# A four-layer graph network on one core: a dense copy of the layer 0 sums, compared numbers in PSUM, twelve gather buffers

## The reference

```python
h = relu(layernorm(x)); x = x + L0(h)   # recv = segment_sum(edge_attr, dst); relu([recv, h, u] @ W1 + b1) @ W2 + b2, 1024 hidden
h = relu(layernorm(x)); x = x + L1(h)   # attention over the edges of a node (max, exp, sums)
h = relu(layernorm(x)); x = x + L2(h)   # degree-scaled sums of node rows, once forward and once backward, two 128x128 products
h = relu(layernorm(x)); x = x + L3(h)   # sums of edge_weight * h[src] by dst, mean, product, layer norm, relu
```

## Time and profile before

| | us |
|---|---|
| median of three runs | 9123.56 (9121.67 to 9123.86) |
| the profiled execution | 9116.86, its span 9115.2 |
| nodes of layer 0 | about 1765 to 2610 |
| layer 2 forward, gathers | 5384 to 6177 |
| layer 2 backward, gathers | 6783 to 7452 |
| layer 3, gathers | 8205 to 8904 |
| PE, DVE, ACT, POOL busy | 7221, 6414, 3251, 4580 |

### The profile page before, as it was taken

One profiled execution on the slowest core, in us unless ns is written; L12 is line 12 of the kernel. 1 busy time (PEld: TensorE's weight loads), 2 busy tenths in 40 slices (PEclk: granted clock), 3 DMA queues, 4 the chain that ended last, 5 costly groups with the idle time before them and its releaser, 6 DMA issues. The chain is left out here.

```text
span 9115.2 us, 230332 instructions
## 1 busy us (share of the span) xinstructions
PE 7221.3 (79%) x60850; PEld 5827.1 (64%) x60851; DVE 6414.1 (70%) x20871; ACT 3251.0 (36%) x9379; POOL 4580.0 (50%) x5503
## 2 busy tenths in 40 slices
PE   4855577799968888888887987776987775997777
PEld 4755566544446666666676766665876664886665
DVE  5999888611147777777776776666776666876667
ACT  3533322222223333333334530005640015668881
POOL 2000477100037777777733557773557752557771
PEclk7985799899977777777788999998999997999996
DMA  0000366400014444444435876676766654776663
GB/s 22 2 2 1 96 140 140 114 23 24 25 48 107 106 107 105 107 105 106 106 121 194 290 237 192 190 179 204 280 244 191 193 169 165 282 281 175 184 184 102
DMA packets 645064, 1262.09 MB, mean 138 GB/s; under 512 B 126526, under 2 KB 183433, under 8 KB 644569
## 3 DMA queue, kind: packets, MB, share of 16 engines
q1 hardware_dynamic: 424337, 704.50, 23.6%
q0 software_dynamic: 199040, 544.46, 22.4%
q10 hardware_dynamic: 21452, 10.20, 0.4%
HBM read 780.96 MB, written 477.75 MB: 138 GB/s over the span
## 5 line engine op out<-in xcount | busy, mean ns | idle before, releaser
L1063 PE MATMUL PS<-w,GS 128*128 128x128 f32 x12176 | 1636.6, 283 | 499.8 <-DVE AREA L1008 229.0
L1063 PEld LDWEIGHTS PS<-w,GS 128*128 128x128 f32 x12176 | 1457.8, 192 | 678.9 <-DVE w L967 444.5
L1171 POOL DMA_INDIRECT GS<-t1d,KI x1564 | 1492.7, 954 | 488.0 <-issue 461.5
L1188 POOL DMA_INDIRECT GS<-xbuf,KI x964 | 1028.4, 1067 | 360.9 <-issue 173.6
L967 DVE TENSOR_TENSOR w<-IO,KI 128x512 f32<-128x512 f32 (+1 forms) x1355 | 808.7, 597 | 421.9 <-issue 411.1
L2419 DVE TENSOR_SCALAR AREA<-PS,IP 128x512 bf16<-128x512 f32 x1116 | 837.4, 751 | 219.7 <-PE PS L2429 115.9
L2441 PE MATMUL PS<-AREA 128*128 128x128 bf16 x13392 | 934.7, 220 | 56.4 <-POOL AREA L2399 56.4
L2441 PEld LDWEIGHTS PS<-AREA 128*128 128x128 bf16 x13392 | 843.5, 98 | 196.6 <-issue 66.1
L2399 POOL TENSOR_TENSOR AREA<-AREA,w 128x192 int32<-128x192 int32 x1116 | 547.8, 504 | 615.7 <-PE PS L2441 330.2
L2381 ACT ACTIVATE GS<-PS 128x512 f32<-128x512 f32 x1116 | 666.4, 597 | 393.5 <-PE PS L2441 393.2
L1188 POOL DMA_INDIRECT GS<-pbuf,XR x558 | 594.0, 1065 | 208.1 <-issue 100.5
(11 more groups left out here) (412 smaller groups left out, 13040.0 us busy)
## 6 DMA issues: line engine op xcount, KB each, us to landing
xbuf<-GS SPq DMA_DIRECT2D x1116, 256.0 KB
XR<-in_edge_attr SPq DMA_DIRECT2D x780, 256.0 KB
pbuf<-AREA SPq DMA_DIRECT2D x482, 256.0 KB
GS<-t1d,KI POOLq DMA_INDIRECT x1564
GS<-xbuf,KI POOLq DMA_INDIRECT x964
GS<-pbuf,XR POOLq DMA_INDIRECT x558
AREA<-t2d ACTq DMA_DIRECT2D x121, 64.0 KB
keyd<-AREA POOLq DMA_INDIRECT x482
```

What stands on the lines that cost most here:

```text
L1063: i = e.matmul(PS[:, s % 3, 0:128], feats(s)[0:m, r, 0:D], SELW[s % 3][0:m, width * r:width * r + 128], start=(r == 0), stop=(r == 3))
L1171: e.indirect_dma_start(GS[0:m, s, r, 0:wide], None, table, bass.IndirectOffsetOnAxis(ap=idx[0:m, c:c + 1].bitcast(U32), axis=0)).then_inc( ...
L1188: e.indirect_dma_start(GF[:, 512 * s:512 * s + 512], None, buf, bass.IndirectOffsetOnAxis(ap=idx[:, b:b + 1].bitcast(U32), axis=0)).then_i ...
```

## The change

Three edits. In `l0_nodes` DVE copies a group's 512 strided sums into a dense buffer `AGT` (two of them, in turn), and the products of PE with the first half of `W1` read that buffer. In the summing passes the numbers 0 to 127 are copied once per phase into PSUM bank 7, and `sel` reads them there. The gathers of the summing passes go round 12 slots, six in `GF` as before and six in `R`, and the loops of DVE, PE and ACT run over 12 batches per turn.

```diff
-    def batches(e, nb, step):
+    def batches(e, nb, step, un=UN):
...
-            if s == 0:
-                held[0] = ranges(e, part, it * (2 * UN), 2 * UN)
-            return held[0][2 * s:2 * s + 2]
+            if s % UN == 0:
+                held[0] = ranges(e, part, it * (2 * un) + 2 * s, 2 * UN)
+            return held[0][2 * (s % UN):2 * (s % UN) + 2]
...
+        num = PS[:, 7, 0:width] if not srel else IO[:, 0:width]
+
         def sel(e, s, kl):
-            return e.tensor_tensor(SEL[s % 3], IO[:, 0:width].unsqueeze(1).to_broadcast([128, 4, width]),
+            return e.tensor_tensor(SEL[s % 3], num.unsqueeze(1).to_broadcast([128, 4, width]),
...
+            if not srel:
+                e.tensor_copy(num, IO[:, 0:width])
...
+    GRING = 12
+
+    def gslot(s):
+
+        return GF[:, 512 * s:512 * s + 512] if s < 6 else R[:, 512 * (s - 6):512 * (s - 5)]
...
-                s = b % UN
-                if b >= UN:
-                    e.wait_ge(bd, b - UN + 3)
-                e.indirect_dma_start(GF[:, 512 * s:512 * s + 512], None, buf,
+                s = b % GRING
+                if b >= GRING:
+                    e.wait_ge(bd, b - GRING + 3)
+                e.indirect_dma_start(gslot(s), None, buf,
...
+        AGT = [B0[:, LISTEND + 4096 + 512 * i:LISTEND + 4608 + 512 * i] for i in range(2)]
+        ag = p.sem("ag")
...
+                e.wait_ge(ag, g + 1)
...
-                    e.matmul(PS[:, m % 2, 0:4 * n].rearrange("h (j p) -> h j p", j=4), W1S[:, 0, 128 * m:128 * m + 128],
-                             jp(AB[:, 0, :], g), start=True, stop=False)
+                    e.matmul(PS[:, m % 2, 0:4 * n], W1S[:, 0, 128 * m:128 * m + 128], AGT[g % 2][:, 0:4 * n],
+                             start=True, stop=False)
...
+            def sums(g):
+                n = grows[g]
+                if g >= 2:
+                    e.wait_ge(ph, 8 * (g - 1))
+                e.tensor_copy(AGT[g % 2][:, 0:4 * n].rearrange("f (j p) -> f j p", j=4), jp(AB[:, 0, :], g)).then_inc(ag, 1)
+
...
+            sums(0)
             copy0(0)
             for g in range(NG):
                 if g + 1 < NG:
+                    sums(g + 1)
                     copy0(g + 1)
...
-                  ready, 16, ACC, weight=weight)
+                  ready, 16, ACC, weight=weight, un=GRING)
```

More of the change, by code:

```diff
@@ L925, in gnn, with unit_ranges @@
     NIT = NBF // UN
-    def batches(e, nb, step):
-        n = nb // UN
+    def batches(e, nb, step, un=UN):
+        n = nb // un
         with e.Fori(0, n) as it:
[L931 to L936, removed]
+            for s in range(un):
+                step(it * un + s, s, it, False)
+        for s in range(nb % un):
+            step(n * un + s, s, n, n * un + s == nb - 1)
+    def unit_ranges(e, nb, part, un=UN):
         held = {}
-        n = nb // UN
+        n = nb // un
         def get(b, s, it, last):
@@ L943, in get, with edge_pass @@
                 return ranges(e, part, 2 * b, 2)
-            if s == 0:
-                held[0] = ranges(e, part, it * (2 * UN), 2 * UN)
-            return held[0][2 * s:2 * s + 2]
+            if s % UN == 0:
+                held[0] = ranges(e, part, it * (2 * un) + 2 * s, 2 * UN)
+            return held[0][2 * (s % UN):2 * (s % UN) + 2]
         return get
-    def edge_pass(p, nb, tail, width, part, keys, feats, ready, rstep, ACC, weight=None, count=False, srel=False):
+    def edge_pass(p, nb, tail, width, part, keys, feats, ready, rstep, ACC, weight=None, count=False, srel=False, un=UN):
         acc, mmd, oh, bd, dv, kx = (p.sem(n) for n in ("acc", "mmd", "oh", "bd", "dv", "kx"))
@@ L988, in _ @@
             e.nop().then_inc(acc, 3)
-            get = unit_ranges(e, nb, part)
+            get = unit_ranges(e, nb, part, un)
             if count:
@@ L1038, in step @@
                     i.then_inc(sr, 1)
-            batches(e, nb, step)
+            batches(e, nb, step, un)
             for q, w_ in (((nb - 2) % 3, wq), ((nb - 1) % 3, wp)):
@@ L1176, in gather @@
         return ready
+    GRING = 12
+    def gslot(s):
+        return GF[:, 512 * s:512 * s + 512] if s < 6 else R[:, 512 * (s - 6):512 * (s - 5)]
     def gather_groups(p, bd, buf, idx, nb):
-        ready = [p.sem(f"g{s}") for s in range(UN)]
+        ready = [p.sem(f"g{s}") for s in range(GRING)]
         @p.on("gpsimd")
@@ L1184, in _ @@
             for b in range(nb):
-                s = b % UN
-                if b >= UN:
-                    e.wait_ge(bd, b - UN + 3)
-                e.indirect_dma_start(GF[:, 512 * s:512 * s + 512], None, buf,
+                s = b % GRING
+                if b >= GRING:
+                    e.wait_ge(bd, b - GRING + 3)
+                e.indirect_dma_start(gslot(s), None, buf,
                                      bass.IndirectOffsetOnAxis(ap=idx[:, b:b + 1].bitcast(U32), axis=0)
                                      ).then_inc(ready[s], 16)
-            for s in range(UN):
-                e.wait_ge(ready[s], 16 * ((nb - 1 - s) // UN + 1))
+            for s in range(min(GRING, nb)):
+                e.wait_ge(ready[s], 16 * ((nb - 1 - s) // GRING + 1))
         return ready
@@ L1278, in l0_nodes @@
         H0T = [B0[:, LISTEND + 3072 + 512 * i:LISTEND + 3584 + 512 * i] for i in range(2)]
-        assert LISTEND + 4096 <= NC
+        AGT = [B0[:, LISTEND + 4096 + 512 * i:LISTEND + 4608 + 512 * i] for i in range(2)]
+        ag = p.sem("ag")
+        assert LISTEND + 5120 <= NC
         HT = [HTS[:, 528 * i:528 * i + 528].rearrange("p (j f) -> p j f", j=4) for i in range(2)]
@@ L2671, in aggregate @@
         ready = gather_groups(p, p.sem("bd"), buf, idx, nb)
-        edge_pass(p, nb, 128, 128, part, keys, lambda s: GF[:, 512 * s:512 * s + 512].rearrange("p (r f) -> p r f", r=4),
-                  ready, 16, ACC, weight=weight)
+        edge_pass(p, nb, 128, 128, part, keys, lambda s: gslot(s).rearrange("p (r f) -> p r f", r=4),
+                  ready, 16, ACC, weight=weight, un=GRING)
         for k in ("vector", "tensor"):
```

## The result

| | us |
|---|---|
| before, beside it | 9122.74 (9121.67 to 9123.86, 4 runs) |
| changed | 8960.60 (8957.45 to 8978.58, 4 runs) |
| ratio | 0.9826, 95% interval 0.9809 to 0.9843 |
| profiled execution of the changed kernel | 8957.86, its span 8956.2 |

A forecast was written before the change was run, and what follows sets the result against it. PE was taken to bound layer 0's nodes, POOL's gathers layer 2, with slot waits added in layer 3. Terms 173 - 1 + 61 + 58 + 90 = 381 us off 9116.9 give 8736, median 8742 us; range 8710 to 8860.

The forecast's parts named there:

- the long loop is fetched anew: Rival: DVE's longer loop in the summing passes is refetched each turn and pauses; 8780 to 8855 us, chance 0.17.
- The pause: At the head of DVE's loop turns, a refetch was priced at 2.2 us more per turn.
- The cover: Twelve batches take DVE 13.8 us and POOL 15.1, so 1.3 us of a refetch pause per turn is free.
- The sum: Refetch cost in the summing passes: 0.9 us per turn, 113 us for all three passes, some 38 for one.
- the refetch at its dearest: Upper end of the range: refetched DVE loops in the summing passes bring the kernel to 8860 us at most.
- The rival for slower: Refetch pauses of 4.3 us per turn in all three summing passes eat the whole gain; 9335 at 6 us; chance 0.02.
- Dense sums: Nodes of layer 0: a dense operand saves PE 0.887 us per piece, 173 us, less 1 us for the first copy.
- Numbers in PSUM: Summing passes: one SBUF operand fewer for DVE shortens POOL's gathers to 0.957 us, 0.11 us less per batch, pace 1.257.
- Twelve slots: Summing passes: later gathers come six places earlier, 7.5 us per pass; layer 3 also loses its waits for a slot.
- The forecast's own sum: Whole kernel: all terms together save 381 us, giving a median of 8742 us; chance 0.63.

The follow-up runs named there:

- e13: Changed kernel with 48 one-element memsets on VectorE ahead of the loop of layer 2 backward and 48 ahead of layer 3's; 8732.7 us, ratio 0.9576.
- e9: Changed kernel with 6 memsets on VectorE ahead of the loop of layer 2 backward and 48 ahead of layer 3's; 10630.9 us, one run, beside 10446.6.
- e10: Changed kernel with 120 memsets on VectorE ahead of the loop of layer 2 backward and 68 ahead of layer 3's; 10427.8 us, one run, beside 10446.6.
- e12: Changed kernel with 48 memsets ahead of each loop of layer 2 backward and layer 3, compared numbers read from SBUF again; 10252.6 us, ratio 0.9814.
- e16: Changed kernel with a ring of six buffers and loops of six batches, dense sums and numbers in PSUM kept; 8808.3 us, ratio 0.9661.
- e11: Changed kernel with nine buffers and loops of nine batches, ranges loaded three batches at a time, no memsets; 10348.9 us, ratio 0.9905.
- e14: Changed kernel with nine buffers and loops of nine batches, ranges of all nine in one load; 8941.3 us, ratio 0.9805.

## Why the prediction was wrong

**The step that failed** is the rival "the long loop is fetched anew": "The trace has no such pause; the nearest rows are the idle time at a turn's head, 1.4 us, and at the first entry of a pass, 2.2". The mechanism was named, the queue with its packets too, but it was given 0.17 and three parts of its price were off:

- The pause. It was taken at 2.2 us more per turn for want of a row. The heads of the turns idle 6.6 us in the median, against 1.4 to 1.6 in the same pass of e13: some 5.0 us more. Three of a turn's five packets lie inside the pause, in the turn shown at 6963.4, 6965.3 and 6967.9 us, one after another, which fits blocks that are asked for only when they are missed.
- The cover. "1.3 us of a pause is free" counted DVE's and POOL's times per turn with PE at full clock. A turn takes 20.8 us for POOL's 15.1: 5.7 lost, so nothing of the 5.0 was free. In the turn shown PE runs empty, its granted clock is still at 0.50 for some six microseconds after it has work again, and the comparisons at 6973.42, 6975.12 and 6976.83 are 1.7 us apart where POOL needs 1.257. No run separates the clock's share from that of the pause.
- The sum. One pass was priced "some 38" us; it cost 836.2 - 613.4 = 223. With the pause alone put right, the prediction's own formula gives 40 x (5.0 - 1.3) = 148, an estimate; the other 75 are the cover. The 223 are the whole miss: 8960.6 - 223 = 8738.

The range closed at 8860, "the refetch at its dearest", with 2.2 us as the dearest pause; the forecast plus the true cost of one pass, 8742 + 223 = 8965, lies 105 us above that. The rival for slower asked for a pause of 4.3 us in all three passes; it was longer than that, but in one pass of three. That two passes were spared is a matter of their place, which the prediction did not look at (shown for layer 3 by e9 and e10; no run moved the loop of layer 2 forward); it counted 269 rows in the body, where the compiled loop has 331 instructions.

**Dense sums**: right, sized 172, measured 179 by the first gather of layer 1. A piece went from 2.66 to 1.71 us, 0.95 less where 0.887 was priced; over 192 pieces that would be 12 us, of which 7 are seen. That the copy is hidden is right. What the Trainium skill says of a stride of 4 float32 being free (SBUF — State Buffer, DMA port swizzle) does not hold for this operand of PE; its other clause, two hits per line, agrees with the factor of two, since a step of four float32 leaves one.

**Numbers in PSUM**: right. The gathers' mean went from 1064 and 1079 ns to 957 with no gather above 1054 (the median was 957 before, too), and in e12, with the operand in SBUF, the means are back at 1062 and 1081. e16 against before gives their worth with six slots: 47, 47 and 31 us.

**Twelve slots**: e13 against e16 gives 22, 8 and 54 us. The 7.5 us per pass fit layer 2 backward; in layer 3 the real waits for a slot went, as said, and in layer 2 forward 14 us more came, most of it at the end of the pass, which had been left "as they are": from the 482nd gather to the last it takes 121 us in e16 and 111 in e13.

**The forecast's own sum** of 8742 was right for the mechanism without the fetches: 8733. In part that is luck, since the terms err both ways: the dense sums gave 7 us more than their term and layer 2 forward 8 more, layer 2 backward (669 to 613) 2 less and layer 3 (700 to 614) 4 less.

## What to carry to other kernels

A hardware loop's price depends on its compiled length and on where it lands: at 331 instructions of VectorE the same loop cost 613 or 836 us per pass, and 48 memsets ahead of it decided. So look for packets on the instruction queue inside a loop's stretch before explaining anything else, keep the body short (252 instructions fetched nothing in the three places that e11 and e14 gave them), and treat a gain from a longer unroll as unsafe until every use of it has been looked at. When pricing a pause for which there is no row, add what an idle PE does to its clock, and let the range take several times the nearest row.

## What was not expected of the hardware

- Instructions of VectorE come in blocks of 128 (8 KB packets), and a loop of 331 is kept or fetched anew by its place: 763 us for the pass at a start of 86, 957 at 94. That it is decided by how far the loop reaches into its fourth block is argued.
- A load of values into registers took 849 ns for 12, 1604 for 24, but 1.57 and 4.06 us by turns for 18.
